# Softmax over heads: twelve of 128 denominators are summed by TensorE in place of VectorE

## What is computed

```python
qkv = x @ w_qkv + b_qkv
qkv = qkv.reshape(b, n, 3, N_HEADS, HEAD_DIM)     # 16 heads of 8
qkv = jnp.transpose(qkv, (2, 0, 3, 1, 4))
q, k, v = (qkv[0], qkv[1], qkv[2])
dp = jnp.einsum('bhqd,bhkd->bhqk', q, k) * SCALE
attn = jax.nn.softmax(dp, axis=1)                 # over the heads
w_avg = jnp.einsum('bhqk,bhkd->bhqd', attn, v)
```

## Time and profile before

| | us |
|---|---|
| median of 3 runs | 2133.75 |
| lowest and highest | 2133.57, 2134.24 |
| the profiled execution | 2139.04 |
| its span, first to last instruction | 2137.3 |
| stage 6 in it, first maxima to last | 1229 to 1828.3 |
| PE, DVE, ACT, POOL busy over the span | 87%, 78%, 53%, 45% |
| mean granted TensorE clock | 0.946 |

### The profile page before, as it was taken

One profiled execution on the slowest core, in us unless ns is written; L12 is line 12 of the kernel. 1 busy time (PEld: TensorE's weight loads), 2 busy tenths in 40 slices (PEclk: granted clock), 3 DMA queues, 4 the chain that ended last, 5 costly groups with the idle time before them and its releaser, 6 DMA issues.

```text
span 2137.3 us, 32729 instructions
## 1 busy us (share of the span) xinstructions
PE 1855.7 (87%) x12452; PEld 1203.5 (56%) x12452; DVE 1659.7 (78%) x2131; ACT 1123.6 (53%) x1868; POOL 955.2 (45%) x365
## 2 busy tenths in 40 slices
PE   6899998986888886799999978888888777899998
PEld 4444454455444446577777745555555455677776
DVE  4556555548799998667777599999999999876676
ACT  2344444443533323345555557776777666555554
POOL 3356555622366751101000078888989889400000
PEclk8799999998999998799999999999999999999999
DMA  3111212000200001001010000000001000000000
GB/s 84 31 31 31 53 25 45 2 12 1 50 0 1 0 1 35 20 14 32 30 30 16 1 1 2 1 2 2 2 1 31 2 2 1 31 30 30 15 15 21
DMA packets 35681, 39.14 MB, mean 18 GB/s; under 512 B 5891, under 2 KB 22534, under 8 KB 35526
## 3 DMA queue, kind: packets, MB, share of 16 engines
q1 hardware_dynamic: 34998, 36.01, 6.7%
q10 hardware_dynamic: 528, 1.05, 0.2%
HBM read 21.05 MB, written 1.05 MB: 10 GB/s over the span
## 4 chain that ended last, share of the span: by engine, by line
PE 50%; DVE 19%; issue 19%; POOL 7%; ACT 4%; DMA 1%; SPq 0%; DVEq 0%; ACTq 0%; POOLq 0%; PEldq 0%
PE ps L46 9%; PE ps L47 8%; PE ps L48 8%; DVE negm L2661 6%; PE ps L530 4%; PE ps L546 3%; PE ps L571 2%; PE ps L579 2%; DVE AF L2668 2%; POOL AF L1572 2%; POOL hc L1572 1%; POOL AR_plain L2466 1%; PE ps L2490 1%; PE ps L2573 1%; DVE AF L823 1%
## 5 line engine op out<-in xcount | busy, mean ns | idle before, releaser
L2661 DVE TENSOR_REDUCE negm<-ps 128x64 bf16<-128x1024 f32 x256 | 303.6, 1224 | 20.3 <-PE ps L2564 20.2
L2466 POOL TENSOR_TENSOR AR_plain<-AF 128x2048 f32<-128x2048 f32 x64 | 261.9, 4095 | 31.4 <-ACT AF L2617 31.3
L753 POOL TENSOR_TENSOR AF<-AF 128x2048 f32<-128x2048 f32 (+3 forms) x52 | 184.5, 3549 | 197.0 <-ACT AF L693 195.1
L46 PE MATMUL ps<-XH,AR 128*128 128x512 f32 x616 | 255.2, 414 | 14.7 <-DVE XL L251 4.0
L2625 ACT ACTIVATE AF<-ps 128x1024 f32<-128x1024 f32 x192 | 196.5, 1023 | 133.5 <-PE ps L2573 132.2
L48 PE MATMUL ps<-XH,AR 128*128 128x512 f32 x616 | 245.7, 399 | 0.0
L47 PE MATMUL ps<-XL,AR 128*128 128x512 f32 x616 | 245.5, 399 | 0.0
L693 ACT ACTIVATE AF<-ps 128x512 f32<-128x512 f32 (+1 forms) x304 | 155.1, 576 | 157.1 <-PE ps L533 72.0
L2573 PE MATMUL ps<-negm,ident_bf 128*128 128x512 bf16 x512 | 161.4, 398 | 80.7 <-DVE negm L2661 80.2
L2668 DVE TENSOR_REDUCE AF<-AF 128x128 f32<-128x2048 f32 x96 | 219.4, 2286 | 0.0
L285 POOL TENSOR_SCALAR var_eps<-mv 128x8 f32<-128x8 f32 x10 | 4.2, 423 | 371.1 <-DVE mv L262 371.0
(11 more groups left out here) (338 smaller groups left out, 4389.5 us busy)
## 6 DMA issues: line engine op xcount, KB each, us to landing
AR<-AR SPq DMA_DIRECT2D x96, 128.0 KB, 2.4
AF<-in_L_ffn_Wg_dram SPq DMA_DIRECT2D x21, 256.0 KB, 2.7
AF<-in_L_ffn_Wu_dram SPq DMA_DIRECT2D x21, 256.0 KB, 3.1
AF<-in_L_ffn_Wd_dram SPq DMA_DIRECT2D x21, 256.0 KB, 3.8
AF<-AF SPq DMA_DIRECT2D x16, 64.0 KB, 2.4
AF<-AR_plain SPq DMA_DIRECT2D x16, 64.0 KB, 2.4
AF<-in_L_attn_a_Wq_dram SPq DMA_DIRECT2D x1, 512.0 KB, 4.0
AF<-in_L_attn_a_Wout_dram SPq DMA_DIRECT2D x1, 512.0 KB, 8.9
```

Source lines behind the costliest of these rows:

```text
L46: pe.matmul(out, ah, bh, start=start, stop=False)
L753: pool.tensor_tensor(zacc[u % 2][:, :, c0:512], zacc[u % 2][:, :, c0:512], pt[t % 4][:, :, 0:w], ALU.add).then_inc(s0_zp, 1)
L2466: pool.tensor_tensor(p6[m % 3].rearrange("p (j q i) -> p j q i", j=HJ, i=2), e6[m % 4].rearrange("p (j q i) -> p j q i", j=HJ, i=2), w6i[: ...
L2661: dve.tensor_reduce(negm6[:, j % 4, :], bank(2 * (j % 3), 2).rearrange("p (j q i) -> p q j i", j=HJ, i=2), mybir.AxisListType.XY, ALU.max, ...
```

## The change

A table `PE_SUM_AT` names twelve tiles whose denominators PE makes. It maps the tile `at`, in whose `pv` the work stands, to the tile m = at + 3 that is summed:

59: 62, 61: 64, 77: 80, 91: 94, 93: 96, 99: 102, 101: 104, 107: 110, 109: 112, 115: 118, 117: 120, 123: 126.

For these, `head_sum` stands on PE after the first half of `pv(at)`: 16 fp32 matmuls, one for each head, with the identity as weights and the head's 128 x 128 exponentials as moving operand, accumulated in `spare_bank(at)`. DVE skips `denominators(m)`. ACT waits for `s6_zq` in place of `s6_zs` and reads the sum from PSUM. `pv` of the next group's first tile waits until ACT has read it.

```diff
+        BUSY_AT = {at + i for at in list(JOBS_AT) + list(LN_AT) for i in (-1, 0, 1, 2)}
+        PE_SUM_AT = {LB * g + kb: LB * g + kb + LAG - 1 for g in range(7, NB) for kb in (3, 5)
+                     if LB * g + kb not in BUSY_AT and LB * g + kb + LAG - 1 < NTI - 1}
+        PE_SUM = {m: at for at, m in PE_SUM_AT.items()}
...
+        def head_sum(pe, m):
+
+            at = PE_SUM[m]
+            wait(pe, s6_st, jobs_before(at))
+            pe.wait_ge(ln_lo, 4 * 6 + 2 + sum(1 for t in LN_AT if t < at))
+            pe.wait_ge(x_done, X_AFTER[6] + at // LB)
+            wait(pe, s6_wi, max([t + 1 for t, other in PE_SUM.items() if other < at], default=0))
+            pe.wait_ge(s6_e, 2 * m + 2)
+            heads = e6[m % 4].rearrange("p (j q i) -> p j q i", j=HJ, i=2)
+            for h in range(H6):
+                ins = pe.matmul(spare_bank(at)[:, 0:P], ident[:, :], heads[:, h // 2, :, h % 2],
+                                start=h == 0, stop=h == H6 - 1)
+            ins.then_inc(s6_zq, 1)
...
                     pv(pe, j // 2 - LAG, j % 2)
+                    if j % 2 == 0 and j // 2 - LAG in PE_SUM_AT:
+                        head_sum(pe, PE_SUM_AT[j // 2 - LAG])
...
-                act.wait_ge(s6_zs, m + 1)
+                if m in PE_SUM:
+                    act.wait_ge(s6_zq, summed(m, True))
+                else:
+                    act.wait_ge(s6_zs, summed(m, False))
                 wait(act, s6_wi, m)
-                link(act.activation(lnz, z6[:, m % 2, :], ACT.Ln))
+                link(act.activation(lnz, spare_bank(PE_SUM[m])[:, 0:P] if m in PE_SUM else z6[:, m % 2, :], ACT.Ln))
...
-                    denominators(j // 2 - 1)
+                    if j // 2 - 1 not in PE_SUM:
+                        denominators(j // 2 - 1)
```

More of the change, by code:

```diff
@@ L2200, in build @@
         s6_zs = sem("s6_zs")
+        s6_zq = sem("s6_zq")
         s6_wi = sem("s6_wi")
@@ L2227, in build, with summed @@
         SCATTER_AT = {LB * (g - 2) + 2 * i: (g, i) for g in range(2, NB) for i in range(HS)}
+        BUSY_AT = {at + i for at in list(JOBS_AT) + list(LN_AT) for i in (-1, 0, 1, 2)}
+        PE_SUM_AT = {LB * g + kb: LB * g + kb + LAG - 1 for g in range(7, NB) for kb in (3, 5)
+                     if LB * g + kb not in BUSY_AT and LB * g + kb + LAG - 1 < NTI - 1}
+        PE_SUM = {m: at for at, m in PE_SUM_AT.items()}
+        def summed(m, by_pe):
+            return sum(1 for t in range(m + 1) if (t in PE_SUM) == by_pe)
         def jobs_before(t):
@@ L2486, in pv @@
                     pe.wait_ge(x_done, X_AFTER[6] + max(g - 1, 0))
+                    wait(pe, s6_wi, max([t + 1 for t, at in PE_SUM.items() if at < m], default=0))
             for x in (2 * part, 2 * part + 1):
@@ L2694, in s6_dve @@
             denominators(NTI - 1)
-            dve.wait_ge(s6_zs, NTI)
+            dve.wait_ge(s6_zs, summed(NTI - 1, False))
             dve.wait_ge(s6_pp, NTI - 2)
```

## The result

| | before | after | ratio, 95% interval |
|---|---|---|---|
| first comparison, median us | 2133.99 | 2161.17 | 1.0125 [1.0104, 1.0146] |
| second comparison, on another run of both | 2136.00 | 2157.25 | 1.0110 [1.0085, 1.0135] |
| profiled execution | 2139.04 | 2157.07 | |
| stage 6, first to last maxima, from the profiles | 599.4 | 622.8 | |

The account below looks back on a forecast made before the run. DVE was taken to set stage 6's pace; twelve sums at X - 1.61 = 1.99 us give +23.9, profiled 2139.04 to 2162.9 and median 2133.75 to 2157.7 us. Range of 8 in 10: 2146 to 2170.

Parts of the forecast that it names:

- Passes: PE's added fp32 matmuls in stage 6: two passes each, so 32 passes a sum, at 0.109 us each.
- rival of four full passes: PE's new sums: four passes of 0.109 us per fp32 matmul, 7.0 us a sum, +65 us, 2198; chance 2%.
- X: PE's time for one added sum, from its start to what follows: taken as 3.6 us, between 3.48 and 3.70.
- one pass with plain fp32: PE's new sums: identity matmuls in one pass, 1.84 us a sum, +2.8 us, 2136.5, not slower; chance 8%.
- the projection's row: Stage 6 projection on PE, 8 passes in 1.09 us: 0.87 for passes, 0.22 for switching from `pv` and back.
- The chain of 7.30 + X: Stage 6, PE and DVE steps through a pair of tiles with a sum: 7.30 + X us against 8.91 before.
- The 1.61 us: Stage 6, subtracted from X for each summed tile's cost: DVE's 2.20 us come off, 0.6 goes back in waiting.
- at most 26.4 us: Twelve DVE sums of 2.20 us removed in stage 6, an upper limit if DVE alone set the pace everywhere.
- PE's idle time takes part of it: Rival, stage 6: PE alone bounds the pair, 9.80 against 8.91 us, +0.89 a sum, +10.7, 2144.4; chance 12%.
- the projection's rate: Rival, PE's sums at 0.136 us a pass: X = 4.36, +33.0 us, 2166.8, or 2170 with two clock falls; chance 15%.
- The last sum: Tile 126, at stage 6's end: DVE 2 to 3 us later there, charged at 2.0 like the others.
- the clock: PE's clock falls in stage 6: added work brings no new ones, may remove three, at most 5 us.

Follow-up runs that it names:

- late: The changed kernel with PE's twelve sums behind the second half of `pv` instead of the first: 2154.09 us, ratio 1.0089 to the kernel before.

## Why the prediction was right

**What bounds the kernel.** Right for the kernel before: DVE waits for nobody, a tile is 4.455 us, and the pairs without a sum keep that to the hundredth after the change.

**Passes.** Right: 384 records for 192 matmuls, two each. The rival of four full passes (X = 7.0) is out, and so is that of one pass with plain fp32; one pass needs fp32r operands and was shown with them. The Trainium skill's four passes (FP8 and Floating Point Precision, TensorE Precision Notes) don't show as records. A plain fp32 sum takes 3.74 us and an fp32r sum 1.92, so it costs about twice as much here. Whether a record of 0.113 us holds two inner passes no run here tells.

**X.** 3.74 us, where I took 3.6 and gave 3.48 to 3.70 as near bounds. The term was 4% short, and X lies just above the bounds. The 0.109 us of a pass was a mean over a run whose last step is short: in the trace 31 of its passes are 0.108 to 0.112 us from start to start, and the last is 0.030. The new run has no such short step. Its passes are 0.113 us, the last 0.115, and the first, behind `pv`, 0.221. So the whole cost of the switch stands in the first step and is 0.11 us, half of the 0.22 that the projection's row left.

**The chain of 7.30 + X.** Right, to 0.02 us, at three values of X. The pair is 11.02, its excess 2.11 against 1.99. DVE's wait is 4.08 us where about 4 was said, the short and long tile 2.39 and 8.63 where 2.4 and 8.5 were said.

**What the 1.61 us are.** Here the text was loose. It said that DVE's 2.20 us come off and 0.6 goes back. The experiment with DVE's sums kept shows that the same 7.30 + X holds with them: at X = 3.74 nothing comes off. The 1.61 us are 8.91 - 7.30, the slack that this chain through PE and DVE already had in the kernel before, and the sum that was taken away is not in the chain. It counts only as long as DVE's own work is the longer one, 8.91 us for a pair with both sums; by these two lengths that ends at X = 1.61, and no run kept the sums at an X near it. The number was right, its name wrong; and the text put "at most 26.4 us" as removed without saying that the likely part of it was zero.

**PE's idle time takes part of it.** The rival at +0.89 a sum, +10.7 in all, did not come about in this place, for the reason given against it. It is about what the later place gives. There, behind the second half of `pv`, two sums of a group take five tiles to 2.39 + 6.89 + 3.16 + 6.88 + 4.91 = 24.23 us against 22.28, +0.98 each, and the second pair, 10.04 us, is PE alone: 4 x 1.58 + 3.74 = 10.06.

**The other rivals and edits.** All twelve X are 3.74 us: no pass came at the projection's rate and no fall of the clock hit a sum. The new line never waited for a semaphore (its idle time, 2.7 us over twelve runs, is all issue), so its waits cost nothing, as the text said.

**The last sum and the clock.** The last sum cost 2.3 us at DVE, as said, but nothing in the end, which the text hadn't said: it charged it at 2.0 like the others, and the next stage's shorter delays took it up. That is luck. So two misses offset each other: with the measured X the prediction's own sum is 12 x 2.13 = 25.6 us, and the stage's 23.4 has eleven sums in it. The clock fell in the stage three times after 1490, as before (in tiles 76 or 77, 93 and 101), none on a sum. The first fall lasted 6.8 us in place of 3.4 and the pair behind it is 0.28 us longer; the other two cost nothing more than before. By the Trainium skill (TensorE: Matmul & The Clock Gate, HAM oscillation) gaps in TensorE's work throttle its clock and a loop without them keeps it up. The trace neither bears that out nor speaks against it, since the falls lie where no sum stands: 0.96 in the same stretch of 1690 to 1730, before and after.

## What to carry to other kernels

Moving work off the busiest engine is worth what it does to the length of one period, and not the work's own length: draw the chain over one period with the new work in its place, and check whether the engine that was relieved now waits longer than what it was relieved of. Work on an in-order engine belongs behind the last instruction that the busiest engine will need, here behind the second half of `pv` and not between its halves; that alone halved the cost in the stage, though part of it came back behind the stage, and with sums of half the length it turned +4 into -7 us in the stage. Leaving the old work in beside the new is a cheap test of whether the saving exists.

## What the runs showed of the hardware

The DVE product with two SBUF operands (line 1356), 0.68 us in nearly all its 128 places behind the stage, took 2.28 us from 1837.25 and 3.98 from 1840.06 in the kernel before, 2.95 from 1860.13 in the changed one, and 4.18 in `late`. Each time it ended 0.55 us behind the end of the POOL product that was running: at 1839.53 beside 1834.89 + 4.09 = 1838.98, at 1844.04 beside 1843.49, at 1863.07 beside 1862.52, and at 1851.53 beside 1850.98:

```profile
1846.90 4.08 POOL L2475 TENSOR_TENSOR AR_plain<-XN,AF 128x2048 f32<-128x2048 f32 x1
1847.35 4.18 DVE L1356 TENSOR_TENSOR AF_rounded<-AR_plain,AF_rounded 128x512 fp32r<-128x512 f32 x1
```

The sums and maxima, with one operand, ran beside the same POOL products at their usual length. The Trainium skill states this rule (SBUF — State Buffer, SBUF: two separate sides): a DVE instruction with two SBUF inputs and a GpSimd instruction that reads SBUF exclude each other for the whole of the one that came first. The trace agrees in these rows. It is the reason why the stage's end is worth a look of its own when POOL's last products are shifted: these delays come to 4.9 us in the kernel before (1.60 + 3.30), 2.3 in the changed one and 3.5 in `late`.
